# Weighing the values of all 16 heads in one block a batch, with 16 places for the transposed probabilities

## What is computed

```
query = layernorm(x) @ w_q.T + b_q;  key_ = ctx @ w_k.T + b_k;  value = ctx @ w_v.T + b_v
scores = einsum('bhqd,bhkd->bhqk', query, key_) / sqrt(32)        # 16 heads of width 32
attn = softmax(where(causal, scores, -inf))
x = x + tanh(g_xattn) * (einsum('bhqk,bhkd->bhqd', attn, value) @ w_o.T + b_o)
x = x + tanh(g_ffn) * (mx_quantize(layernorm(x)) @ mx_quantize(weight).T + bias)
```

## Time and profile before

| | |
|---|---|
| median of 3 runs | 1406.31 us (1406.27 to 1407.74) |
| the profiled execution, its own time | 1405.65 us |
| its span, first to last instruction | 1403.9 us |
| busy share of the span | PE 97%, PE's weight loads 87%, DVE 77%, ACT 64%, POOL 62% |
| mean granted TensorE clock | 0.99 of full speed |
| DMA | 159.11 MB, 113 GB/s, 42.5% of the 16 engines' time |

### The profile page before, as it was taken

One profiled execution on the slowest core, in us unless ns is written; L12 is line 12 of the kernel. 1 busy time (PEld: TensorE's weight loads), 2 busy tenths in 40 slices (PEclk: granted clock), 3 DMA queues, 4 the chain that ended last, 5 costly groups with the idle time before them and its releaser, 6 DMA issues.

```text
span 1403.9 us, 35217 instructions
## 1 busy us (share of the span) xinstructions
PE 1368.0 (97%) x10844; PEld 1221.2 (87%) x10844; DVE 1085.5 (77%) x4219; ACT 896.8 (64%) x2969; POOL 867.0 (62%) x1387
## 2 busy tenths in 40 slices
PE   6899999999999999999999999999999999999987
PEld 6789988899888898898898988889998888998875
DVE  5777787887787887778777778878778878778774
ACT  4666666666666666666667666666666566666562
POOL 1556765566665576665566666566666566666564
PEclk9999999999999999999999999999999999999998
DMA  8444344444334444434444434454434444434320
GB/s 254 112 112 116 88 115 118 120 128 114 98 102 122 118 125 117 111 95 121 118 128 118 112 90 119 118 131 119 111 89 121 118 125 123 112 97 112 88 68 31
DMA packets 156616, 159.11 MB, mean 113 GB/s; under 512 B 28688, under 2 KB 131088, under 8 KB 156432
## 3 DMA queue, kind: packets, MB, share of 16 engines
q1 hardware_dynamic: 156432, 156.88, 42.0%
HBM read 39.33 MB, written 16.78 MB: 40 GB/s over the span
## 4 chain that ended last, share of the span: by engine, by line
PE 91%; SPq 3%; DVE 2%; issue 1%; DMA 1%; POOL 1%; ACT 1%; DVEq 0%; ACTq 0%; POOLq 0%
PE proj L511 20%; PE proj L512 20%; PE proj L513 20%; PE pT_ps L572 12%; PE proj L588 6%; PE proj L615 6%; PE s_ps L561 4%; PE s_ps L562 2%; SPq L360 2%; DMA all_probs<-in_L_xattn_w_v 1%; DMA q_stack<-q_hi 0%; DMA k_stack<-k_lo 0%; POOL xs_yz L472 0%; POOL xs_yz L476 0%; ACT all_probs L691 0%
## 5 line engine op out<-in xcount | busy, mean ns | idle before, releaser
L437 POOL TENSOR_TENSOR all_probs<-all_probs,rden 128x128 f32<-128x128 f32 (+1 forms) x1024 | 517.6, 526 | 445.9 <-DVE rden L895 444.5
L691 ACT ACTIVATE all_probs<-all_probs,neg_max 128x128 f32<-128x128 f32 (+1 forms) x1024 | 458.8, 451 | 373.0 <-DVE neg_max L837 372.7
L837 DVE CUSTOM_DVE_ANT_0 all_probs<-s_ps,causal 128x128 f32<-128x128 f32 (+1 forms) x1024 | 323.6, 353 | 195.7 <-PE s_ps L562 190.0
L572 PE MATMUL pT_ps<-ident,all_probs 128*128 128x128 f32 x1536 | 264.4, 282 | 7.8 <-POOL all_probs L437 4.0
L691 ACT ACTIVATION_READ_ACCUMULATOR all_probs<-all_probs,neg_max 128x1 f32 x1024 | 195.4, 191 | 0.0
L959 DVE COPY all_probs<-pT_ps 128x384 f32<-128x384 f32 x256 | 139.2, 544 | 53.8 <-PE pT_ps L572 53.5
L572 PEld LDWEIGHTS pT_ps<-ident,all_probs 128*128 128x128 f32 x1536 | 160.4, 142 | 22.8 <-issue 12.5
L561 PE MATMUL s_ps<-k_stack,q_stack 96*128 96x256 f32 x512 | 154.5, 302 | 3.3 <-DVE neg_max L837 2.2
L511 PE MATMUL proj<-cT_hi,wk_hi 128*128 128x256 f32 x512 | 153.6, 300 | 0.0
L511 PE MATMUL proj<-aT_hi,wq_hi 128*128 128x256 f32 x512 | 148.6, 290 | 0.0
L512 PE MATMUL proj<-aT_lo,wq_hi 128*128 128x256 f32 x512 | 142.9, 279 | 0.0
(11 more groups left out here) (114 smaller groups left out, 3465.1 us busy)
## 6 DMA issues: line engine op xcount, KB each, us to landing
k_stack<-k_hi SPq DMA_DIRECT2D x512, 64.0 KB, 2.0
q_stack<-q_hi SPq DMA_DIRECT2D x512, 64.0 KB, 2.1
xs_yz<-in_x SPq DMA_DIRECT2D x32, 512.0 KB, 4.5
cs<-in_ctx SPq DMA_DIRECT2D x32, 512.0 KB, 5.9
k_stack<-k_lo SPq DMA_DIRECT2D x256, 64.0 KB, 2.0
q_stack<-q_lo SPq DMA_DIRECT2D x256, 64.0 KB, 2.1
out<-xs_yz SPq DMA_DIRECT2D x64, 256.0 KB, 2.3
vs<-in_L_xattn_w_k SPq DMA_DIRECT2D x2, 512.0 KB, 7.0
```

The costliest lines, as they stand in the source:

```text
L437: last = nc.gpsimd.tensor_tensor(p, p, rden[:, sd, t, h:h + 1].to_broadcast([P, (1 + t) * P]), ALU.mult)
L572: last = nc.tensor.transpose(pT_ps[h % 2][:, m * P:(m + 1) * P], probs[:, h % P_RING, m * P:(m + 1) * P], ident[:, :])
L691: last = nc.scalar.activation(probs[:, h % P_RING, cols], probs[:, h % P_RING, cols], ACT.Exp, scale=-1.0, bias=neg_max[:, sd, t, h:h + 1] ...
L837: last = nc.vector.tensor_tensor_reduce(probs[:, h % P_RING, cols], s_ps[h % 2][:, cols], causal[:, (1 - t) * P:], 1.0, MASKED, ALU.add, A ...
```

## The change

Both blocks of a batch now stand together, in slot 3 of step b+3: 32 calls in one go, each half of them in a bank of its own. `probsT` has 16 places, one a head; the copy of a head waits for the block of the batch before. ACT's and DVE's `output_hi` and `output_lo` of both follow in slot 4. The units' parts are dealt anew: the fourth part of `k` of half 0 goes from slot 3 to slot 2, so that this unit ends one slot earlier; slot 3 holds no unit. Slot 10 gives a part of `q` of half 0 to slot 11, which also gets another part of `v`; slot 14 keeps only two parts of `v` of half 1, and `k` of half 1 ends in slot 13.

```
-AV_SLOTS = (11, 3)
-AV_STEPS = (2, 3)
+AV_SLOT = 3
+AV_STEPS = 3
...
-SLOT_PARTS = (2, 4, 4, 1, 1, 5, 4, 2, 3, 4, 4, 1, 3, 3, 3, 2)
+SLOT_PARTS = (2, 4, 5, 0, 1, 5, 4, 2, 3, 4, 3, 3, 3, 3, 2, 2)
...
-            taken += [("av", r, i - AV_STEPS[r]) for r in range(2) if s == AV_SLOTS[r] and live(i - AV_STEPS[r])]
+            if s == AV_SLOT and live(i - AV_STEPS):
+                taken += [("av", r, i - AV_STEPS) for r in range(2)]
...
-        all_probs = sb("all_probs", [P, P_RING + AV_HEADS, 3 * P])
+        all_probs = sb("all_probs", [P, P_RING + HEADS, 3 * P])
...
-            def weigh_values(b, r, sd):
-
-                pe.wait_ge(pT_even, 8 * b + 4 * r + 4)
-                pe.wait_ge(pT_odd, 8 * b + 4 * r + 4)
+            def weigh_values(b, sd):
+
+                pe.wait_ge(pT_even, 8 * b + 8)
+                pe.wait_ge(pT_odd, 8 * b + 8)
 
                 pe.wait_ge(left["v"], 2 * b + 2)
-                free_bank("av", r, b)
-                bank = bank_of("av", r, b)
...
+                for r in range(2):
+                    free_bank("av", r, b)
+                    bank = bank_of("av", r, b)
...
+                                h = AV_HEADS * r + GROUP * half + j
...
+                                    probsT[:, h, 2 * P * kt:2 * P + P * kt], start=kt == 0,
+                                    stop=kt == T - 1, tile_position=(0, j * DK))
+                    last.then_inc(av_done, 1)
...
-                        if some(n := 2 * b + h // AV_HEADS):
-
-                            dve.wait_ge(av_done, n)
-                        nc.vector.tensor_copy(probsT[:, h % AV_HEADS, :], pT_ps[0][:, 0:3 * P]).then_inc(pT_even, 1)
+                        if some(b):
+
+                            dve.wait_ge(av_done, 2 * (b - 1) + h // AV_HEADS + 1)
+                        nc.vector.tensor_copy(probsT[:, h, :], pT_ps[0][:, 0:3 * P]).then_inc(pT_even, 1)
...
-                    for r in range(2):
-                        if s == AV_SLOTS[r] + 1 and live(i - AV_STEPS[r]):
-                            output_lo(i - AV_STEPS[r], r)
+                    if s == AV_SLOT + 1 and live(i - AV_STEPS):
+                        for r in range(2):
+                            output_lo(i - AV_STEPS, r)
```

More of the change, by code:

```diff
@@ L574, in transpose_probs @@
                 last.then_inc(pT_done, 1)
-            def weigh_values(b, r, sd):
-                pe.wait_ge(pT_even, 8 * b + 4 * r + 4)
-                pe.wait_ge(pT_odd, 8 * b + 4 * r + 4)
+            def weigh_values(b, sd):
+                pe.wait_ge(pT_even, 8 * b + 8)
+                pe.wait_ge(pT_odd, 8 * b + 8)
                 pe.wait_ge(left["v"], 2 * b + 2)
-                free_bank("av", r, b)
-                bank = bank_of("av", r, b)
-                for half in range(2):
-                    for kt in range(T):
-                        for j in range(GROUP):
-                            d = (AV_HEADS * r + GROUP * half + j) * DK
-                            last = nc.tensor.matmul(
-                                bank[j * DK:(j + 1) * DK, half * S + kt * P:(half + 1) * S],
-                                vs[:, sd, kt, d:d + DK],
-                                probsT[:, GROUP * half + j, 2 * P * kt:2 * P + P * kt], start=kt == 0,
-                                stop=kt == T - 1, tile_position=(0, j * DK))
-                last.then_inc(av_done, 1)
+                for r in range(2):
+                    free_bank("av", r, b)
+                    bank = bank_of("av", r, b)
+                    for half in range(2):
+                        for kt in range(T):
+                            for j in range(GROUP):
+                                h = AV_HEADS * r + GROUP * half + j
+                                last = nc.tensor.matmul(
+                                    bank[j * DK:(j + 1) * DK, half * S + kt * P:(half + 1) * S],
+                                    vs[:, sd, kt, h * DK:(h + 1) * DK],
+                                    probsT[:, h, 2 * P * kt:2 * P + P * kt], start=kt == 0,
+                                    stop=kt == T - 1, tile_position=(0, j * DK))
+                    last.then_inc(av_done, 1)
             def unit(kind, half, b, part):
@@ L651, in step @@
                         scores(i - 2, s)
-                    for r in range(2):
-                        if s == AV_SLOTS[r] and live(i - AV_STEPS[r]):
-                            weigh_values(i - AV_STEPS[r], r, side(ph, AV_STEPS[r]))
+                    if s == AV_SLOT and live(i - AV_STEPS):
+                        weigh_values(i - AV_STEPS, side(ph, AV_STEPS))
                     lag, b, h = transposed_head(i, s)
@@ L755, in step @@
                         unit(kind, half, of)
-                    for r in range(2):
-                        if s == AV_SLOTS[r] + 1 and live(i - AV_STEPS[r]):
-                            output_hi(i - AV_STEPS[r], r)
+                    if s == AV_SLOT + 1 and live(i - AV_STEPS):
+                        for r in range(2):
+                            output_hi(i - AV_STEPS, r)
                     if live(i - 2):
@@ L764, in step @@
                         act.wait_ge(pT_done, HEADS * b + h + 1)
-                        if some(n := 2 * b + h // AV_HEADS):
-                            act.wait_ge(av_done, n)
-                        nc.scalar.activation(probsT[:, h % AV_HEADS, :], pT_ps[1][:, 0:3 * P],
+                        if some(b):
+                            act.wait_ge(av_done, 2 * (b - 1) + h // AV_HEADS + 1)
+                        nc.scalar.activation(probsT[:, h, :], pT_ps[1][:, 0:3 * P],
                                              ACT.Copy).then_inc(pT_odd, 1)
```

## The result

| | before | after |
|---|---|---|
| median of 6 runs each | 1406.29 us (1406.09 to 1407.74) | 1435.64 us (1434.19 to 1439.62) |
| the profiled execution, its own time | 1405.65 us | 1434.5 us |
| its span | 1403.9 us | 1432.7 us |
| mean granted TensorE clock | 0.990 | 0.988 |

The change makes the kernel slower by 2.1%: after / before is 1.0213 [1.0201, 1.0226]. The prediction said 1435 us, range 1416 to 1452.

What follows compares the result with a forecast made beforehand. PE was taken to bound the kernel, matmuls back to back; -8.7 (block) + 30.5 (new wait) + 4.4 + 3 (SP's queue) = +29 on the profiled 1405.65, forecast 1435 us, range 1416 to 1452.

Steps and rivals of the forecast that it cites:

- doubled block: PE, slot 3: two blocks in one pay entry and exit of 32-column work once, saving 0.28 a batch, -8.7 us.
- wait at `dT` half 1: PE behind slot 3's transposes: waits 1.05 us a step for its bank, released by DVE's `aT_lo`, +30.5 us.
- `k_hi` late, `q_stack` late: Later SP DMAs delay ACT's `k_hi`, +4.4 us, and the next step's slot 0 scores through `q_stack`, +3 us.
- start-up and run-out: Run-out: the last batch's block moves behind all its transposes; put at 0, bounds -2 and +3.
- T: The start of PE's transposes in slot 3, from which the prediction counts times in us.
- the late step: Step of 42.90 us in the kernel before, with one PE wait; used as a price list for waits.
- What is late next: Slots 4 to 6: `f` half 0 at T+2.77 just in time for `k_lo`, `f` half 1 at T+6.49 0.3 in time.
- The margin: Before `f` half 1: PE is released by `aT_lo` half 1 at T+6.16, 0.3 in time.
- rival 3: Emptying bound: ACT's and DVE's added output copies make PE wait also at `f` half 1; +16, 1451 us, chance 0.12.
- The queue of SP: SP's stacking DMAs begin some 1.9 us later, using up 0.85 idle; `k_hi` +4.4 us, `q_stack` +3 us.
- Rival 4: SP bound: late DMA groups make `k_hi` hold every step, 1.1 more in 29 steps; 1467 us, chance 0.06.
- Emptying as the limit: Both blocks' banks emptied in one slot: the skill's PSUM warning speaks against the change, the third rival, chance 0.12.

Runs made afterwards that it cites:

- e7: Changed kernel with `q` half 0 ending in slot 10 and, in slot 3, DVE writing low halves of `dT` and `k` ahead of head 0's copy: 1404.33 us.
- e1: Changed kernel, but in slot 3 DVE writes the low half of `dT` half 0 ahead of its copy of head 0: 1430.82 us.
- e3: Changed kernel with `dT`'s low half ahead of head 0's copy on DVE and `q` half 0 ending in slot 10: 1407.40 us.
- e8: e7 with the doubled block split, half ahead of slot 3's scores and half behind them: 1422.54 us.
- e5: Changed kernel, but the fourth part of `k` half 0 stays in slot 3 as before: 1431.99 us.
- e11: Changed kernel with PE doing slot 3's transposes ahead of the block, `q` half 0 still ending in slot 11: 1429.58 us.
- e10: Changed kernel with PE doing slot 3's transposes ahead of the block and `q` half 0 ending in slot 10: 1399.42 us.
- e9: Kernel before with only DVE's order in slot 3 changed, finished units' low halves ahead of the copy of head 0: 1406.61 us.
- e2: Changed kernel, but `q` half 0 ends in slot 10 again (slots 10 and 11 hold 4 and 2 parts): 1425.70 us.

## Why the prediction was right, point by point

**The time and its sum.** 1435 against 1435.64. The terms, each against what the traces give for it:

| term | predicted | measured, from |
|---|---|---|
| doubled block | -0.28 x 31 = -8.7 | -0.25 x 29 = -7.3 (41.82 to e7's 41.57) |
| wait at `dT` half 1 | 1.05 x 29 = +30.5 | 0.94 x 29 = +27.3 (slot 4: 1.90, against 0.96 in e1, e3 and e7) |
| `k_hi` late, `q_stack` late | +4.4 and +3 | +6.9 (the excess of 0.24 over the ordinary step) |
| start-up and run-out | 0 | -1.8 and +3.4 |
| sum | +29 | +28.5, of a span that grew by 28.8 |

The mechanism was right, and the terms were near. That the total came within 1 us is luck on top: the terms were off by +1.4, -3.2, -0.5 and +1.6, and cancel. The top of the range, 1452, left out the upper bounds of `q_stack` (+8) and of the run-out (+3); with them it would have been 1463.

**The saving.** The 0.28 a batch was 0.25, and the stretch that was to show it, forecast at 3.2, is 3.19. e8's seam of 0.34 is the same thing from the other side. The Trainium skill (TensorEngine Tiling, Key Properties) has the drain at a change of mode: the runs agree that there is a price, 0.25 to 0.34 us for an entry and an exit. The Trainium skill's other page (TensorE: Matmul & The Clock Gate, Single matmul latency), by which an estimate gave 0.33, lies between the two; these runs don't tell its account of the price from another.

**The new wait** stood where it was said to, with the releaser named, 28 times in the stretch shown. Its 1.05 was 0.94, because both ends were a little off. `dT` half 1 starts at T+1.80 rather than T+1.89: the release came 0.74 after the start of `aT_lo`, where the late step had shown 0.83. And without a wait it would start at T+0.91 rather than T+0.84: that is where e3 has it (632.60 to 633.51) with the bank free. These make 0.89; the other 0.05 of slot 4 stands behind the start, where the next scores follow 0.41 after `dT` half 1 (687.65 to 688.06) and in e3 0.35 (633.51 to 633.86). That the moved part uncovers the wait is confirmed by e5: with the part back, 0.3 is left of it. The bounds, 0.75 and 1.2, hold it.

**What is late next.** `f` half 0 at T+2.77, measured T+2.74; `k_lo` at T+1.66, measured T+1.66; `aT_lo` half 1 at T+5.33, measured T+5.34; `f` half 1 at T+6.49, measured T+6.46, without a wait. The margin held in the steps looked at, and no wait of `f` half 1 for `aT_lo` stands in the list; the excess that rival 3 would have put at slot 6 is in slot 5 (mean 3.92, median 3.73), at `f` half 0.

**The queue of SP.** 1.91 nearer as said, the idle 0.85 down to 0.10; ACT's start at T+0.05 in the ordinary step (forecast for a later one: T+1.10) and T+1.49 in the late one. The 4.4 and 3 us for `k_hi` and `q_stack` were 5.0 and 3.1 by the waits of the weight loads, in 7 and 6 steps. What the prediction did not see is that these small sums were small only because the wait at L617 covered the rest: 30 us stood behind it (e11 against e10), the falls of the clock behind long waits among them. Rival 4, the queue holding each step, was priced as an addition, at 1467. It is an alternative: it appears once the other wait is gone, and then gives about the same time, 1430 (e1, e11).

**The run-out** was put at 0 with a bound of +3, and is +3.4 with the steps ahead of the 29 at -1.8. The mean granted clock behind the 29 steps is 0.86 where it was 0.90, so part of it may be clock. What of the rest is the last block behind its transposes and what the last landings stays open.

**Emptying as the limit.** The Trainium skill (TensorEngine Tiling, PSUM Bottleneck) says that the copy out of PSUM may become the limit. In the trace of after PE stands idle at L590 once, 1.4 us, put down to issue and not to an emptied bank, and e10, with the same two banks in one slot, is the fastest kernel of all; this case doesn't show that limit for the blocks. The wait at L617 is one for a bank to be emptied too, but it is `dT`'s bank, and e1 and e10 end the wait by order alone, with the same work of emptying.

## What to carry to other kernels

Joining two blocks saves one entry and exit (0.25 us here) but pushes all that stands behind them on an in-order engine back by a block: look at what the other engines have queued behind the first result from there, and put that small work (here three transposes) ahead of the block. Two lateness chains that end at the same place hide each other, so remove both before judging either: singly they gave 5 to 10 us, together 28 to 36. A wait that is long in one piece can cost more than itself: behind five waits, of 1.75 to 2.19 us, the granted clock fell to 0.50, 1.6 us each. When parts are dealt anew, keep in its slot the one that starts a queue of DMAs which a later step waits for.

## What the runs showed that I had not expected

- The order of DVE's work in one slot was worth nothing in the kernel before (e9: 1406.61 against 1406.3, step 41.83) and 21 us in the changed one (e7 against e2: 1404.3 against 1425.7 with the same table). An order within an engine costs nothing until the engine that waits for it changes its own.
- The longest steps are long for two reasons. With the same DMAs in the same order, e1's longest is 45.17, e5's 45.71 and e11's 45.68 where the change has 43.62; in each of the three the granted clock fell behind PE's wait, 1.6 us a time. In e1's longest step ACT's copy of the key unit starts 13.45 into the step, no later than in the change's longest (13.47). The change spreads its waits, at most 0.7 of idle PE at a time, and no fall stands in its 29 steps. In the mean of the 29 steps that copy starts at 12.29 in the change, 12.35 in e1 and 12.46 in e11 (latest 13.47, 13.66 and 14.06); from one execution each, it is not shown that the landings themselves came later.
- e11's four runs lie in the order of their mean granted clocks: 1425.65 us at 0.989, 1426.81 at 0.987, 1432.35 at 0.984, 1436.44 at 0.983. One fall of 3.41 us to 0.50 takes 0.0012 off that mean and cost 1.6 us, so an estimate from these would make the gap between the first and the last five falls, 8 us. Four runs don't show it, though: e2's runs have means from 0.986 to 0.990 and lie within 1.5 us. Other kernels scatter as well: the 23 runs of the kernel before beside e5 and e7 to e9 lie between 1403.23 and 1411.33.
